# The end of a routing stage: four tiles taken together, and the order of the projections behind them

## The chip, the cores and the metric

The kernel runs on one core of one Trainium2 chip. The metric is the device time of one execution in microseconds (us), the median of several runs; less is better. A core has five engines that work side by side and meet only at semaphores: PE (matmuls and transposes; its weight loads are shown as PEld), DVE (vector), ACT (activations), POOL (here: memsets and storing DMAs) and SP (here: loading DMAs). Each engine runs its own list of instructions strictly in order.

## What is computed

The reference has two layers. The first routes 2048 states of width 256 over 1601 context tokens of width 192, and updates each state through a gated cell; the second is a transformer block (self-attention, cross-attention, MLP) on the result. Cut to what matters here:

```python
# layer 0
tok = ctx @ W_proj + b_proj
attn = softmax(x @ tok.T / 16)
routed = attn @ tok
ps_n, in_n = ln(x), ln(routed)
u = sigmoid([ps_n, in_n] @ W_u + b_u)
r = sigmoid([ps_n, in_n] @ W_r + b_r)
cand = tanh([r * ps_n, in_n] @ W_n + b_n)
x = ln((1 - u) * x + u * cand)
# layer 1
h = ln(x)
q, k, v = h @ Wq.T + bq, h @ Wk.T + bk, h @ Wv.T + bv     # 16 heads of 16
x = x + softmax(q k.T / 4) v @ Wo.T + bo                   # self-attention
x = x + cross_attention(ln(x), ctx)
x = x + gelu(ln(x) @ W1.T + b1) @ W2.T + b2
```

## The kernel before, in words

The 2048 rows are 16 tiles of 128 rows, and four chunks of four tiles. Layer 0 goes over the chunks; for each it computes scores against the 13 context tiles (`l0_scores`), their exponentials (`exps` on ACT), the low parts (`lower` on DVE) and the weighted sum of context (`l0_pv`). All that follows for a tile is a pipeline of stages, each written out by hand in every engine's list, one `slot(k)` for each k from 0 to 22. Tile k-4 is routed and normalised in slot k, tile k-5 goes through the gates and the candidate, tile k-6 is finished, and tile k-7 is normalised for layer 1.

For one tile the path is: `route` (PE, bank 6: the routed row and its softmax sum) → `norms` (DVE: reciprocal, scaling into E1, statistics, a `rsqrt` of twelve small instructions for up to three tiles at once, then the two normalised tiles XHS and XH1) → `hats` (PE: four transposes into bank 3) → `concat` (ACT: CF with scale and bias) → `gates` (PE: r and u into bank 7) → `reset` (ACT: tanh) → `gates` (DVE: UZ, RPS) → `update` (ACT: tanh) and `candidate` (PE, bank 7 again) → CZ (DVE) → `candidate` (ACT: tanh to CD) → the new state E2 with its statistics (DVE) → `finish` in the next slot (DVE) → the `rsqrt` and XH1 one slot later → `h_transposed` (PE, bank 2) → `h_taken` (ACT: hF). TR, RPS, UZ, TU, CZ, CD, E1 and E2 exist once, CF, XHS and XH1 twice.

Once the hF of a chunk's four tiles is there, its q, k and v are projected. `stage3` lists for each chunk ten units: keys of two halves, four v tiles, queries of two halves, and a norm of the keys and one of the queries (`norm`, a product of squares with a matrix of heads). For a q or k unit ACT makes three passes (`split`: two parts and a square), DVE makes the low part (`lower_parts`), and POOL stores both parts to DRAM (`store_parts`), from where SP loads them into the stacked layout of the attention. `qkv_bank` gives a unit its PSUM bank. DENSE, EARLY and LATE say in or behind which slot units stand: chunk 0 behind slot 10, chunk 1 (FIRST) in slots 16 and 17, chunk 2 (SECOND) in slots 19 to 21, chunk 3 behind slot 22. Slots 16 to 22 have no scores left beside the tail of the pipeline.

The self-attention starts after that. Its first scores (PE, `scores`) need the queries with their shift rows: once the key norm of the last chunk is known, DVE computes the shift (`self_shift(0)`, lines 1656, 1657, then `shift_rows`, lines 1518, 1519), POOL stores it (`store_shift`) and SP loads it. They also need `decide(0)`: after the last query norm DVE reduces the norms (L1834, L1835), PE turns the column into a row (L1228), DVE writes a flag (L1838, L1839), and every engine reads this flag into a register and branches on it (`general`). In the attention a pass of 928 exponentials on ACT (L886) and the products on PE (L1308 scores, L1325 values) run with double and triple buffering.

POOL fills half of V with ones in one memset of 4096 columns (L645) once the last `l0_pv` is done; DVE writes features of heads into it later. The lines of the profile are those of this file:

Of the kernel before, what the change touches and what calls it, by code (L numbers as in the profile page):

```python
# [131 lines left out]
def build(nc, ctx, d, out):  # L132
# [87 lines left out]
    TU = m.put("TU", [P, D], F32, oWOP + 3 * D * 4)  # L220
    PS = ctx.enter_context(nc.psum_tensor("PS", [P, 8, CHUNK], F32))
# [21 lines left out]
    AGX, NYX, MXP, NMX = 192, 224, 256, 272  # L243

    def sm(o, n=1, p=P):
# [10 lines left out]
        l0_scores l0_exp l0_lo l0_pv l0_oc l0_routed l0_hat l0_hatT l0_concat  # L256
# [44 lines left out]
    for n in range(CHUNKS):  # L301
        vs = [("v", kt, 0, 0) for kt in range(n * TPC, (n + 1) * TPC)]
        ks, qs = ([(kind, n * CHUNK, CHUNK, mm) for mm in range(2)] for kind in "kq")
        norms = [("norm", CHUNKS + 2 * n + i, CHUNK, 0) for i in range(2)]
        stage3.append([(10 * n + i,) + e for i, e in
                       enumerate(ks + vs[:2] + qs[:1] + norms[:1] + qs[1:] + vs[2:] + norms[1:])])
# [6 lines left out]
    DENSE = {10: 0, 22: 3}  # L313
    FIRST, SECOND = stage3[1], stage3[2]
    EARLY = {16: FIRST[0:4], 17: FIRST[8:10], 21: SECOND[8:10]}
    LATE = {16: FIRST[4:8], 19: SECOND[0:4], 20: SECOND[4:8]}
    SLOTS = TILES + TPC + 3
# [34 lines left out]
    def part_buffer(u):  # L352
# [5 lines left out]
        return PARTS[:, mm], S[f"parts_stored{mm}"], n  # L358

# [251 lines left out]
    def _(gp):  # L611
# [37 lines left out]
        for i in range(CHUNKS):  # L649
            store_shift(i, 0, i * CHUNK)  # L650
# [15 lines left out]
    def _(act):  # L666
        def split(u, bank, w, mm, bias):


            wait(act, S["parts_ready"], u - 1)  # L670
# [95 lines left out]
        def reset(i):  # L766

            act.wait_ge(S["l0_gates"], i + 1)
            wait(act, S["l0_rps"], i)
            for c in range(2):  # L770
                ins = act.activation(TR[:, c, :], PS[:, 7, c * P:(c + 1) * P], ACT.Tanh, bias=sm(BRH + c), scale=0.5)  # L771
            ins.then_inc(S["l0_rtanh"], 1)

        def update(i):

            act.wait_ge(S["l0_ubiased"], i + 1)
            act.activation(TU[:], UZ[:], ACT.Tanh, scale=0.5)

        def state_hat(i):
# [5 lines left out]
            act.activation(XHS[:, i % 2, 0, :], X[:, i, :], ACT.Identity, scale=sm(NYX + i), bias=sm(NMX + i))  # L785

        def concat(i):

            act.wait_ge(S["l0_hatT"], i + 1)
            for k, (g_, b_) in enumerate(2 * [("L0_xattn_g_state", "L0_xattn_beta_state")]  # L790
                                         + 2 * [("L0_xattn_g_input", "L0_xattn_beta_input")]):
                ins = act.activation(CF[:, i % 2, k, :], PS[:, 3, k * P:(k + 1) * P], ACT.Identity,  # L792
# [3 lines left out]
        def candidate(i):  # L796

            act.wait_ge(S["l0_candz"], i + 1)
            act.activation(CD[:], CZ[:], ACT.Tanh).then_inc(S["l0_cand"], 1)

        def slot(k):
# [4 lines left out]
            if b >= CHUNKS:  # L806
                if k == TILES:
                    routed_out(b - 1)
                if g is not None:
                    reset(g)  # L810
                qkv(EARLY.get(k, ()))
                if g is not None:
                    update(g)
                state_hat(tile_at(k, 3))
                if r is not None:
                    concat(r)
                if g is not None:
                    candidate(g)
                qkv(LATE.get(k, ()))
                if h is not None:  # L820
                    h_taken(h)
                return
# [26 lines left out]
            else:  # L849
                if j == TPC - 1 and b + 1 < CHUNKS:  # L850
                    shift_row(b + 1)
                state_hat(tile_at(k, 3))
# [7 lines left out]
        for k in range(SLOTS):  # L860
            slot(k)
            if k in DENSE:
                qkv(stage3[DENSE[k]])

# [56 lines left out]
    def _(pe):  # L921
# [164 lines left out]
        def route(i):  # L1086
# [6 lines left out]
            wait(pe, S["l0_hat"], i)  # L1093
            pe.matmul(PS[:, 6, 0:D + 1], OC[:, 0, tt * P:(tt + 1) * P], WN[:, 0, :], start=True, stop=False)
            pe.matmul(PS[:, 6, 0:D + 1], OC[0:SUM + 1, 1, tt * P:(tt + 1) * P], WN[0:SUM + 1, 1, :],
                      start=False, stop=True).then_inc(S["l0_routed"], 1)

        def hats(i):

            pe.wait_ge(S["l0_hat"], i + 1)  # L1100
            take(3, S["l0_concat"], i + 1)
            for k in range(4):
                ins = pe.transpose(PS[:, 3, k * P:(k + 1) * P], XHS[:, i % 2, k // 2, (k % 2) * P:(k % 2 + 1) * P],  # L1103
                                   ident[:])
            ins.then_inc(S["l0_hatT"], 1)

        def gates(i):

            pe.wait_ge(S["l0_concat"], i + 1)
            wait(pe, S["l0_candz"], i)  # L1110
            for mm in range(2):
                for c in range(4):
                    pe.matmul(PS[:, 7, mm * P:(mm + 1) * P], W0[:, 1, c, mm * P:(mm + 1) * P], CF[:, i % 2, c, :],  # L1113
                              start=(c == 0), stop=(c == 3))
            for c in range(4):
                ins = pe.matmul(PS[:, 7, D:2 * D], CF[:, i % 2, c, :], W0[:, 0, c, :], start=(c == 0), stop=(c == 3))  # L1116
            ins.then_inc(S["l0_gates"], 1)

        def candidate(i):
# [3 lines left out]
            pe.wait_ge(S["l0_rps"], i + 1)  # L1123
            for c in range(4):
                ins = pe.matmul(PS[:, 7, 0:D], RPS[:, c, :] if c < 2 else CF[:, i % 2, c, :], W0[:, 2, c, :],  # L1125
                                start=(c == 0), stop=(c == 3))
            ins.then_inc(S["l0_candps"], 1)

        def slot(k):
# [4 lines left out]
            if b >= CHUNKS:  # L1134
                if k == TILES:
                    for i in range(LAG):
                        l0_pv(n - LAG + i)
                    route(r)
                if g is not None:
                    gates(g)  # L1140
                qkv(EARLY.get(k, ()))
                if r is not None:
                    hats(r)
                if g is not None:
                    candidate(g)
                if tile_at(k, 3) is not None:
# [946 lines left out]
```

## Time and profile before

| | us |
|---|---|
| three runs | 1520.23, 1520.31, 1516.40 |
| their median | 1520.23 |
| the profiled execution, whole | 1512.68 |
| its span on the core | 1511.0 |
| mean granted PE clock in it, of full speed | 0.968 |
| last `l0_pv` of layer 0 issued | 322.4 |
| first score product of the self-attention | 435.24 |

All times of rows count from the start of the span. The span has a first part (layer 0 at full pace, up to about 322 us), the stretch from 322 to 435 us that holds slots 16 to 22 with the last projections, and the attentions with the MLP from 435 us on. In the rows a bracket after an instruction is the idle time of its engine just before it, and what ended that. PS is the whole PSUM, so the line tells which bank is meant; names that end in a number in the code have lost it in the rows (E is E1 or E2, XH is XH1).

### The profile page before, as it was taken

The page shows a single profiled execution, that of the slowest core. Times are in us where ns is not written, and L with a number is a line of the kernel's source. Part 1 is how long each engine was busy: PE and PEld are TensorE (multiplying, and loading weights), DVE is VectorE, ACT ScalarE, POOL GpSimd, SP SyncE. Part 2 cuts the span into 40 slices and gives each one's busy share as a digit, 9 for nine tenths or more (in the row PEclk, how much of TensorE's full clock was granted, in tenths as well). Part 3 has the DMA queues.
Part 4 walks back from the last instruction along what each step waited for, and adds up shares of the span by engine and source line. Part 5 has one row for each costly group of instructions (what it writes and reads, how often), then busy time and mean ns, then how long its engine had stood idle before and what let it go on. Part 6 is the DMA issues. An engine that isn't in the chain of part 4 may idle for free.

```text
span 1511.0 us, 20524 instructions
## 1 busy us (share of the span) xinstructions
PE 1409.6 (93%) x7934; PEld 623.1 (41%) x7934; DVE 567.5 (38%) x1343; ACT 1094.8 (72%) x1346; POOL 48.7 (3%) x63
## 2 busy tenths in 40 slices
PE   7989899996679999999999998998999999999988
PEld 5668676775422223223222322322323432432347
DVE  5557575777540113303322231440431233143132
ACT  2543444453359999998999998888877787788842
POOL 2000000010010000000000000000000000000000
PEclk9999999998789999999999999999899999999998
DMA  9410001001269000100100353501000000000000
GB/s 298 164 37 1 1 1 56 1 29 51 88 125 148 22 13 12 39 14 15 34 28 12 44 119 48 122 29 47 12 12 15 22 12 12 22 15 1 4 11 14
DMA packets 35048, 66.05 MB, mean 44 GB/s; under 512 B 6203, under 2 KB 20093, under 8 KB 34205
## 3 DMA queue, kind: packets, MB, share of 16 engines
q1 hardware_dynamic: 29580, 43.24, 13.3%
q0 software_dynamic: 5360, 21.37, 3.9%
q8 instruction: 69, 1.13, 0.3%
q14 instruction: 39, 0.31, 0.1%
HBM read 42.70 MB, written 22.02 MB: 43 GB/s over the span
## 4 chain that ended last, share of the span: by engine, by line
PE 67%; ACT 21%; DVE 6%; issue 3%; DMA 2%; SPq 0%; DVEq 0%; POOL 0%; ACTq 0%; POOLq 0%
PE PS L1325 20%; ACT PX L886 19%; PE PS L1308 14%; PE PS L1376 4%; PE PS L1386 3%; PE PS L1361 2%; PE PS L1113 2%; PE PS L1125 2%; PE PS L1116 2%; PE PS L1042 2%; PE PS L1081 1%; PE PS L1082 1%; PE PS L1083 1%; PE PS L1344 1%; PE PS L1459 1%
## 5 line engine op out<-in xcount | busy, mean ns | idle before, releaser
L886 ACT ACTIVATE PX<-PS 128x1024 f32<-128x1024 f32 (+1 forms) x928 | 882.6, 1039 | 136.0 <-PE PS L1308 87.9
L1325 PE MATMUL PS<-PX,V 128*32 128x512 f32 (+1 forms) x3712 | 500.7, 612 | 5.0 <-ACT PX L886 3.0
L1308 PE MATMUL PS<-QST,stack 50*128 50x512 f32 (+1 forms) x1856 | 386.0, 474 | 19.6 <-issue 13.7
L1308 PEld LDWEIGHTS PS<-QST,stack 50*128 50x128 f32 (+1 forms) x1856 | 157.0, 185 | 417.5 <-ACT PX L886 335.5
L1882 DVE COPY OT<-PS 128x512 f32<-128x512 f32 x32 | 22.1, 691 | 310.5 <-PE PS L1325 309.3
L1325 PEld LDWEIGHTS PS<-PX,V 128*32 128x32 f32 (+1 forms) x3712 | 73.9, 108 | 151.3 <-issue 129.3
L755 ACT ACTIVATE PH<-PS 128x512 fp32r<-128x512 f32 (+1 forms) x52 | 31.2, 600 | 79.4 <-PE PS L1062 69.3
L1386 PE MATMUL PS<-W,HIDT 128*128 128x256 f32 x192 | 51.5, 414 | 9.8 <-ACT HIDT L872 9.8
L1376 PE MATMUL PS<-HC,W 128*128 128x512 f32 x96 | 53.2, 641 | 0.0
L1909 DVE RECIPROCAL REC<-REC 128x256 f32<-128x256 f32 x30 | 52.6, 1753 | 1.0
L771 ACT ACTIVATE TR<-PS,small 128x128 f32<-128x128 f32 x32 | 10.0, 363 | 56.7 <-PE PS L1116 56.7
L1386 PEld LDWEIGHTS PS<-W,HIDT 128*128 128x128 f32 x192 | 36.5, 200 | 34.5 <-issue 30.0
L1954 DVE TENSOR_SCALAR HIDT<-PS,cols 128x512 f32<-128x512 f32 x24 | 18.0, 751 | 79.9 <-PE PS L1376 79.8
L1694 DVE TENSOR_TENSOR PL<-PEXP,PH 128x512 fp32r<-128x512 f32 (+1 forms) x52 | 35.8, 689 | 27.2 <-ACT PEXP L756 26.1
L1081 PE MATMUL PS<-PH,CN 128*128 128x512 f32 (+1 forms) x104 | 43.2, 416 | 0.9 <-DVE PL L1694 0.9
L1932 DVE TENSOR_TENSOR XH<-PS,rows 128x256 f32<-128x256 f32 x28 | 11.9, 425 | 81.2 <-PE PS L1361 81.2
L1082 PE MATMUL PS<-PH,CN 128*128 128x512 f32 (+1 forms) x104 | 41.5, 399 | 0.0
L1083 PE MATMUL PS<-PL,CN 128*128 128x512 f32 (+1 forms) x104 | 41.4, 398 | 0.0
L1587 DVE TENSOR_REDUCE small<-PS 128x1 f32<-128x512 f32 x64 | 35.1, 570 | 8.2 <-PE PS L963 7.4
L1959 DVE TENSOR_TENSOR XH<-PS,rows 128x256 f32<-128x256 f32 x12 | 5.1, 425 | 78.2 <-PE PS L1386 78.2
L1042 PE MATMUL PS<-hF,SAW 128*128 128x512 f32 x64 | 31.5, 627 | 2.0 <-ACT hF L736 2.0
L792 ACT ACTIVATE CF<-PS,cols 128x128 f32<-128x128 f32 x64 | 24.0, 456 | 10.6 <-PE PS L1103 10.6
(194 smaller groups left out, 1461.6 us busy)
## 6 DMA issues: line engine op xcount, KB each, us to landing
QST<-q_parts SPq DMA_DIRECT2D x192, 64.0 KB
q_parts<-PARTS POOLq DMA_DIRECT2D x16, 512.0 KB, 3.6
stack<-k_parts SPq DMA_DIRECT2D x24, 200.1 KB, 6.7
stack<-k_parts SPq DMA_DIRECT2D x18, 256.0 KB
k_parts<-KPARTS POOLq DMA_DIRECT2D x8, 512.0 KB, 3.2
v_cross<-V POOLq DMA_DIRECT2D x1, 3328.0 KB, 12.3
V<-v_cross SPq DMA_DIRECT2D x2, 1664.0 KB, 13.7
k_parts<-PARTS POOLq DMA_DIRECT2D x6, 512.0 KB, 3.4
```

The costliest lines, as they stand in the source:

```text
L886: act.activation(PX[0:kr, (2 * t + half) % 4, :, :], PS[0:kr, slot:slot + 2, :], ACT.Exp, scale=SCALE).then_inc(at["exp"], 1)
L1042: ins = pe.matmul(PS[:, bank, :], SAW[:, "qk".index(kind), c, mm * P:(mm + 1) * P], hF[:, c, at:at + w], start=(c == 0), stop=(c == 1))
L1081: pe.matmul(PS[0:w, bank, :], c_hi, hi, start=first, stop=False)
L1082: pe.matmul(PS[0:w, bank, :], c_lo, hi, start=False, stop=False)
L1083: ins = pe.matmul(PS[0:w, bank, :], c_hi, lo, start=False, stop=last)
L1308: ins = pe.matmul(PS[0:kr, 2 * (n % LOOK) + jj, :], KST[a][lo:lo + NROW, pair, kt * P:kt * P + kr].bitcast(F32R), QST[lo:lo + NROW, pair, ...
L1325: ins = pe.matmul(PS[32 * j:32 * j + 32, 6, :], V[0:kr, kt, 2 * (g // 2 * GH + j) + g % 2, :], PX[0:kr, (2 * t + j // 2) % 4, j % 2, :], s ...
L1376: ins = pe.matmul(PS[:, 7, :], (CAWQ if kind == "u" else W1)[:, c, i * P:(i + 1) * P], HC[:, c, :], start=(c == 0), stop=(c == 1))
L1386: ins = pe.matmul(PS[:, 7, 0:D], HIDT[:, k, i * P:(i + 1) * P], W2[:, k, :], start=(k == 0), stop=(k == HID // P - 1))
L1587: ve.tensor_reduce(sm(MXP + tt * len(pcs) + p), PS[:, max_bank(m), 0:pcs[p][1]], AX, ALU.max) \
L1694: ve.tensor_tensor(PL[0:kr, n % RING, :].bitcast(F32R), PEXP[0:kr, n % RING, :], PH[0:kr, n % RING, :], ALU.subtract).then_inc(S["l0_lo"], 1)
L1909: ch(ve.reciprocal(part, part))
```

## The change

The slots 16 to 22 are gone; in their place each engine has a list `last_tiles()`, in which the four tiles 12 to 15 go through each step together or closely behind each other.

- Tiles 12 to 15 get buffers of their own (CF4, XHS4, TR4, RPS4, TU4, CD4, E4), and banks of their own: routed rows in 6, 4, 5, 3 and gates in 6, 4, 5, 7.
- DVE takes statistics of the four routed rows straight from PSUM (`routed_stats`), folds the softmax sum into the scale with small instructions (`routed_scales`, one `rsqrt` over six columns), and ACT makes the four normalised rows (`routed_hat`) in the order 15, 12, 13, 14. The later `rsqrt`s run over one, one, four and four columns.
- DVE's list puts units of chunks 1 and 2 between the tiles' steps; PE's list too. Chunk 2's units use banks 4, 5, 6, 7, 1, 0 and the rest three or six banks instead of four.
- In every chunk the norm of the keys now stands ahead of both query units; DVE takes the last chunk's key norm and the shift before its v tiles, and the first shift skips one copy (L1656). POOL stores this shift ahead of the last queries.
- POOL's memset of half of V is now eight memsets, of the columns that DVE doesn't write, behind a wait for `l0_scaled`; DVE waits for each by itself.
- ACT's `split` no longer waits for `parts_ready`.

```diff
-            ks + vs[:2] + qs[:1] + norms[:1] + qs[1:] + vs[2:] + norms[1:]
+            ks + vs[:2] + norms[:1] + qs + vs[2:] + norms[1:]
-        return (0, 1, 2, 3)[u % 4] if u < 10 else (0, 1, 4, 5)[u % 4]
+        if u < 10:
+            return (0, 1, 2, 3)[u % 4]
+        return (u - 10) % 3 if u < 20 else (4, 5, 6, 7, 1, 0)[(u - 20) % 6]
 # POOL
-                gp.memset(V[:, TILES // 2:TILES], 1.0).then_inc(S["v_cleared"], 1)
+                gp.wait_ge(S["l0_scaled"], 1)
+                for n in range(TILES // 2, TILES):
+                    gp.memset(v_parts(n, P)[:, :, 1:3, :], 1.0).then_inc(S["v_cleared"], 1)
 ...
+                if half and i == CHUNKS - 1:
+                    store_shift(0, 0, 0)
 # ACT
+        def routed_hat(i):
+            j = i - FIRST_LAST
+            act.wait_ge(S["l0_scaled"], 1)
+            act.activation(XHS4[:, j, 1, :], PS[:, route_bank(i), 0:D], ACT.Identity, scale=sm(SC4 + j),
+                           bias=sm(SB4 + j)).then_inc(S["l0_hat"], 1)
+        def last_tiles():
+            a, b, c, e = LASTS
+            routed_out(CHUNKS - 1)
+            reset(a - 1)
+            update(a - 1)
+            for i in LASTS:
+                state_hat(i)
+            qkv(FIRST[0:2])
+            h_taken(a - 3)
+            for i in (e, a, b, c):
+                routed_hat(i)
+            candidate(a - 1)
+            concat(a)
+            concat(b)
 ...
+            qkv(SECOND)
+            for i in LASTS:
+                h_taken(i)
+            qkv(THIRD)
 # PE
+        def last_tiles():
+            a, b, c, e = LASTS
+            for i in range(LAG):
+                l0_pv(STEPS - LAG + i)
+            gates(a - 1)
+            for i in LASTS:
+                route(i)
+            candidate(a - 1)
+            qkv(FIRST[0:2])
+            h_transposed(a - 3)
+            qkv(FIRST[2:5])
+            hats(a)
+            hats(b)
+            gates(a)
+            hats(c)
+            gates(b)
+            candidate(a)
+            h_transposed(a - 2)
+            hats(e)
+            gates(c)
+            h_transposed(a - 1)
+            candidate(b)
+            gates(e)
+            qkv(FIRST[5:6])
+            candidate(c)
+            qkv(FIRST[6:8])
+            candidate(e)
+            qkv(FIRST[8:])
+            qkv(SECOND[0:8])
+            for i in LASTS:
+                h_transposed(i)
+            qkv(SECOND[8:])
+            qkv(THIRD)
 # DVE
+        def routed_stats(i):
+            j = i - FIRST_LAST
+            ve.wait_ge(S["l0_routed"], i + 1)
+            ch(ve.reciprocal(sm(RS4 + j), PS[:, route_bank(i), D:D + 1]))
+            stats(PS[:, route_bank(i), 0:D], j, ch, STAT4, AG4)
+        def last_tiles():
+            norms(None, a - 2, a - 3)
+            finish(a - 2, into=four[5])
+            gates(a - 1)
+            for i in LASTS:
+                routed_stats(i)
+            routed_scales()
+            next_hat(a - 2, AG4 + 10, NY4 + 5)
+            candidate_sum(a - 1)
+            new_state(a - 1, four[4])
+            rsqrt4(1, 4)
+            finish(a - 1, AG4 + 8, NY4 + 4, four[6])
+            gates(a)
+            qkv(FIRST[0:4])
+            gates(b)
+            candidate_sum(a)
+            qkv(FIRST[4:5])
+            new_state(a, four[0])
+            rsqrt4(1, 6)
+            next_hat(a - 1, AG4 + 12, NY4 + 6)
+            gates(c)
+            candidate_sum(b)
+            new_state(b, four[1])
+            gates(e)
+            candidate_sum(c)
+            qkv(FIRST[5:6])
+            new_state(c, four[2])
+            candidate_sum(e)
+            qkv(FIRST[6:8])
+            new_state(e, four[3])
+            rsqrt4(TPC)
+            finish(a, AG4, NY4, four[0])
+            qkv(FIRST[8:])
+            finish(b, AG4 + 2, NY4 + 1, four[1])
+            qkv(SECOND[0:2])
+            finish(c, AG4 + 4, NY4 + 2, four[2])
+            finish(e, AG4 + 6, NY4 + 3, four[3])
+            rsqrt4(TPC)
+            next_hat(a, AG4, NY4)
+            next_hat(b, AG4 + 2, NY4 + 1)
+            qkv(SECOND[2:5])
+            next_hat(c, AG4 + 4, NY4 + 2)
+            next_hat(e, AG4 + 6, NY4 + 3)
+            qkv(SECOND[5:])
+            qkv(THIRD[0:2] + THIRD[4:5] + THIRD[2:4] + THIRD[5:])
```

Here a, b, c, e are tiles 12, 13, 14, 15; `candidate_sum` is the addition that makes CZ, `new_state` the three instructions that make E2 and its statistics, `next_hat` the one that makes XH1.

## Rows read from the trace of the kernel before

**Rows 1.** The page: busy time of two engines, and PE's granted clock in 40 slices.
```profile
DVE  5557575777540113303322231440431233143132
...
PEclk9999999998789999999999999999899999999998
```

**Rows 2.** Windows: stretch, its length, busy time of PE, PEld, DVE, ACT, POOL; clock; DMA.
```profile
322.40:435.20 112.80, 76.45 (x318) 52.79 (x316) 73.80 (x226) 42.15 (x91) 13.24 (x15) 0.86 0.23 77
...
388.00:398.00 10.00, 8.29 (x32) 5.22 (x31) 6.90 (x17) 3.95 (x9) 1.45 (x2) 1.00 0.28 105
...
404.00:411.00 7.00, 2.15 (x6) 0.87 (x6) 5.19 (x19) 1.19 (x4) 1.42 (x2) 0.50 0.78 237
```

**Rows 3.** Timeline of DVE (start, us, engine, line, operation): one tile's period.
```profile
354.50 0.42 DVE L1746 TENSOR_TENSOR CZ<-PS,rows 128x256 f32<-128x256 f32 x1 [1.27 <-PE PS L1125]
355.48 0.42 DVE L1750 TENSOR_TENSOR E<-CD,X 128x256 f32<-128x256 f32 x1 [0.55 <-ACT CD L799]
...
357.75 0.17 DVE L1701 RECIPROCAL small<-PS 128x1 f32<-128x1 f32 x1
357.95 0.48 DVE L1702 TENSOR_SCALAR E<-PS,small 128x256 f32<-128x256 f32 x1
...
359.38 0.17 DVE L1496 TENSOR_SCALAR small<-small 128x3 f32<-128x3 f32 x1
...
361.77 0.41 DVE L1709 TENSOR_SCALAR XHS<-E,small 128x256 f32<-128x256 f32 x1
...
362.67 0.42 DVE L1723 TENSOR_TENSOR UZ<-PS,rows 128x256 f32<-128x256 f32 x1
...
363.59 0.48 DVE L1734 SCALAR_TENSOR_TENSOR E<-E,small,rows 128x256 f32<-128x256 f32 x1
...
367.19 0.43 DVE L1746 TENSOR_TENSOR CZ<-PS,rows 128x256 f32<-128x256 f32 x1 [1.70 <-PE PS L1125]
```

**Rows 4.** Timeline of DVE: its work for projected units, and the last XH1.
```profile
392.52 1.42 DVE L1536 TENSOR_TENSOR KPARTS<-KPARTS 128x512 fp32r<-128x512 f32 x2
...
404.84 0.75 DVE L1683 TENSOR_TENSOR V<-PS,rows 128x256 f32<-128x256 f32 x2
405.62 0.68 DVE L1672 COPY NQ<-PS 16x512 f32<-16x512 f32 x1
...
409.36 0.41 DVE L1714 TENSOR_SCALAR XH<-X,small 128x256 f32<-128x256 f32 x1
```

**Rows 5.** Timeline of PE: gates, candidates and the last keys, with idle time before them.
```profile
363.61 2.07 PE L1125 MATMUL PS<-W,RPS 128*128 128x256 f32 x4 [0.71 <-DVE RPS L1725]
...
386.99 1.89 PE L1116 MATMUL PS<-W,CF 128*128 128x256 f32 x8
390.60 1.13 PE L1125 MATMUL PS<-W,RPS 128*128 128x256 f32 x4 [1.71 <-DVE RPS L1725]
...
411.57 5.08 PE L1042 MATMUL PS<-hF,SAW 128*128 128x512 f32 x8 [1.05 <-ACT hF L736]
```

**Rows 6.** Timelines of DVE, PE, POOL: flag and first scores, twice, and the shift.
```profile
430.43 0.14 DVE L1839 TENSOR_SCALAR flag<-small 1x1 int32<-1x1 f32 x1
...
435.24 1.65 PE L1308 MATMUL PS<-QST,stack 50*128 50x512 f32 x6 [5.04 <-issue]
...
938.30 0.14 DVE L1839 TENSOR_SCALAR flag<-small 1x1 int32<-1x1 f32 x1
...
943.13 1.65 PE L1308 MATMUL PS<-QST,stack 50*128 50x512 f32 x6 [5.06 <-issue]
...
428.79 0.52 POOL L630 DMA_DIRECT2D shift<-Rp  x1 [0.26 <-issue]
```

**Rows 7.** Timeline of ACT: taking a transposed tile, and the first key pass of chunk 3.
```profile
410.62 0.81 ACT L736 ACTIVATE hF<-PS,cols 128x128 f32<-128x128 f32 x2 [4.12 <-PE PS L1024]
414.98 0.69 ACT L674 ACTIVATE KPARTS<-PS,cols 128x512 f32<-128x512 f32 x1 [3.55 <-PE PS L1042]
```

**Rows 8.** Timeline of POOL: the memset of half of V.
```profile
322.83 3.51 POOL L645 MEMSET V<- 128x4096 f32 x1 [82.52 <-PE PS L1083]
```

**Rows 9.** Windows: the start of the self-attention, columns as in rows 2.
```profile
435.00:500.00 65.00, 64.06 (x402) 18.86 (x402) 6.30 (x12) 62.61 (x68) 1.01 (x2) 0.95 0.82 130
```

More of the change, by code:

```diff
@@ L858, in slot @@
                 h_taken(h)
-        for k in range(SLOTS):
+        for k in range(TILES):
             slot(k)
@@ L1133, in slot @@
             n = LT * b + (3 * j + 1 if j else 0)
[L1134 to L1146, printed above, removed]
-                    route(r + 1)
-                qkv(LATE.get(k, ()))
-                if h is not None:
-                    h_transposed(h)
-                return
             if j == 0:
@@ L1207, in slot @@
             maxima(5)
-        for k in range(SLOTS):
+        for k in range(TILES):
             slot(k)
@@ L1726, in gates, with finish @@
                                     op0=ALU.add, op1=ALU.mult).then_inc(S["l0_rps"], 1)
             ve.wait_ge(S["l0_rps"], g + 1)
-        def finish(f):
+        def finish(f, mean=AG, y=NY, into=(2, STAT, AG)):
             if f is None:
                 return
-            xt = X[:, f, :]
-            ch(ve.scalar_tensor_tensor(out=E2[:], in0=E2[:], scalar=sm(AG), in1=row("L0_xattn_g_out"),
+            xt, e2 = X[:, f, :], work_of(f)[6]
+            ch(ve.scalar_tensor_tensor(out=e2, in0=e2, scalar=sm(mean), in1=row("L0_xattn_g_out"),
@@ new lines, in candidate_sum, with new_state @@
+        def candidate_sum(g):
+            ve.wait_ge(S["l0_candps"], g + 1)
+            ve.tensor_tensor(work_of(g)[4], PS[:, gate_bank(g), 0:D], row("L0_xattn_b_n"), ALU.add) \
+                .then_inc(S["l0_candz"], 1)
+            ve.wait_ge(S["l0_candz"], g + 1)
+        def new_state(g, into=(0, STAT, AG)):
+            ve.wait_ge(S["l0_cand"], g + 1)
+            _, _, _, tu, _, cd, e2 = work_of(g)
+            xt = X[:, g, :]
+            ch(ve.tensor_tensor(e2, cd, xt, ALU.subtract))
+            ch(ve.scalar_tensor_tensor(out=e2, in0=tu, scalar=1.0, in1=e2, op0=ALU.add, op1=ALU.mult))
+            ch(ve.scalar_tensor_tensor(out=e2, in0=e2, scalar=0.5, in1=xt, op0=ALU.mult, op1=ALU.add))
+            i, st, ag = into
+            stats(e2, i, ch, st, ag)
@@ new lines, in last_tiles @@
+        def last_tiles():
+            a, b, c, e = LASTS
+            four = [(j, STAT4, AG4) for j in range(7)]
+            norms(None, a - 2, a - 3)
[22 more added lines that the diff above has]
+            candidate_sum(c)
+            qkv(FIRST[5:6])
+            new_state(c, four[2])
[17 more added lines that the diff above has]
+            qkv(THIRD[0:2] + THIRD[4:5] + THIRD[2:4] + THIRD[5:])
@@ L1759, in slot @@
             n = LT * b + (3 * j + 1 if j else 0)
-            if b >= CHUNKS:
-                norms(r, f, h)
-                gates(g)
-                finish(f)
-                qkv(LATE.get(k - 1, ()))
-                qkv(EARLY.get(k, ()))
-                candidate(g)
-                return
             if j == 0:
@@ L1818, in slot @@
                 x_stats((None, range(6, 12), range(12, 16))[k])
-        for k in range(SLOTS):
+        for k in range(TILES):
             slot(k)
```

190 lines of the change are left out of this document (121 added, 69 removed).

## The prediction

> **What bounds the kernel now.** I read the page first: DVE is busy to 0.5 or more in the first slices only, and PE's clock is whole nearly everywhere [rows 1]; so most of the span is not what this change touches. The windows then show the stretch that it does: 322.4 to 435.2 us, 112.8 us, in which PE is busy 76 us, DVE 74 and ACT 42 [rows 2]. No engine is full: the stretch is a dependence chain that changes hands. DVE's timeline shows the pace. From one CZ to the next is 367.19 - 354.50 = 12.7 us, and inside one period DVE waits only where it handed work to PE or ACT and has its sole buffer in play (0.55 and 1.70 us) [rows 3]. All in all DVE idles 16.0 us between 323.05 (its first instruction of slot 16) and 409.77 (end of the last XH1 [rows 4]); the other 70.7 us it works, with its gaps of 0.03 us counted in. Then come the keys of chunk 3, 411.57 [rows 5], and the first scores, 435.24 [rows 6].
>
> What ends that last piece isn't what the chain of waits names, the load of the shift. Between flag and first scores lie 435.24 - 430.57 = 4.67 us at the self-attention, and 943.13 - 938.44 = 4.69 us at the cross-attention, where no shift was late [rows 6]. Two equal gaps: the flag, which each engine reads into a register and branches on, opens the attention. The shift only has to be in time.
>
> **The change, part by part.** The sum follows DVE's new list from 323.05 on, since DVE has the most work in it. Prices, each a difference of starts [rows 3]: new_state 357.75 - 355.48 = 2.27; a rsqrt 361.77 - 359.38 = 2.39; XH1 0.45; gates 363.59 - 362.67 = 0.92; finish 1.94 (as 2.27 without one operation, its two being 0.48 long); CZ 0.45; reciprocal with statistics 359.38 - 357.75 - 0.50 = 1.13, as the scaling of 0.48 goes. Units: low part 0.72, v tile 0.38, key norm 0.71, query norm 1.42 [rows 4].
>
> 1. DVE's work up to XH1 of tile 15. Six rsqrts (14.3), seven XH1 (3.15), six finishes (11.6), five gates (4.6), four routed statistics (4.5), four small scaling instructions (0.8), five CZ (2.25), five new states (11.4), and of chunks 1 and 2: six low parts (4.3), six v tiles (2.3), two key norms (1.4) and one query norm (1.4). Sum 62.0 us, against 70.7. The 8.7 that go: four scalings into E1 (2.0), four XHS that ACT makes now (1.8), one rsqrt (2.4), less the four small ones (0.8), is 5.4; about 3.6 is only moved (two low parts, two v, a query norm of chunk 2 behind XH1).
>
> 2. DVE's waits. I walked the three lists side by side with these prices, PE's gates at 3.5 us and a candidate at 1.73 (eight of 0.215 at full clock), a q or k unit at 1.72, concat 1.5, each of ACT's split 1.73. Waits that remain: 2.6 us before the new state of tile 11 (ACT stands in its split of two keys, tile 9 and four hats, then tanh); 0.3 and 0.9 at the gates of 12 and 13; 1.2 and 0.6 around CZ and tanh of 13, because PE holds its candidate behind h_transposed(11), which waits for DVE's XH1 of tile 11; 1.0 at the gates of 15; 1.8 and 0.9 at CZ of 14 and 15, where a query unit runs ahead of the candidate. Sum 9.3 against 16.0. PE idles 2.2 us before candidate 13. After an idle of 1.71 us the four products took 1.13, while behind 3.3 us and then 0.71 us they took 2.07 [rows 5]; 2.2 is nearer to the first, so I add 0.4 (ends 0 and 1.8). XH1 of tile 15 then ends at 323.05 + 62.0 + 9.3 + 0.4 = 394.8, 15.0 us earlier.
>
> 3. From there to chunk 3's keys. Four transposes share bank 2, so each waits for ACT to take the one before: 0.65 + 0.81 + 0.05 = 1.5 us [rows 7]. The first can start at 392.0, the fourth ends at 397.1, and ACT has it at 398.0. PE then issues two units of chunk 2 ahead of the keys, up to 2.7 us at the half clock; that spell would have cost k (5.08 us for two instead of 3.44 [rows 5]), so the keys come out as if started at 398.5. That is 3.7 us behind XH1 against 1.8: +1.9 us.
>
> 4. Chunk 3 up to the scores, 23.7 us before. Key norm and shift move ahead of the v tiles and the queries, one copy of 0.46 goes. Queries start one norm later (+0.3 at ACT) and DVE has no shift between q0 and q1. The last query norm hangs on ACT's square of q1 and comes out 2.0 us earlier: -2.0. Shift ready at +10.5, and by the row of POOL [rows 6] 6.45 us more plus 0.6 makes +17.6, under the flag's +21.6.
>
> Sum: -15.0 + 1.9 - 2.0 = -15.1 us.
>
> **At nothing.** Dense chunk 0: its norm waits for ACT's second key square either way; its q0 comes out 0.1 us later. POOL: its one memset took 3.51 us for 4096 columns [rows 8], and eight of 256 are 1.8 us; the new wait for the scales starts them near 336.5, and behind it on POOL stands the store of chunk 1's keys, ready near 349. Without this cover, 1.8 us at most. SP may load the first key quarters some 38 us earlier, since the last routed product moves from slot 19's end to 330; nobody waits for them. The dropped parts_ready wait of ACT is implied by the store's.
>
> The Trainium skill speaks against the memsets' place. SBUF — State Buffer, section "SBUF: two separate sides", says that DVE's two-port modes and GpSimd lock each other out for a whole instruction. XH1 of tile 10 is a tensor_scalar in SBUF and falls beside them. By that rule it would be late by one small piece, an estimate below 0.5 us, swallowed by the 2.6 us wait that follows; no row here shows such a lock.
>
> **The rivals.**
> (B) The handoffs cost more than walked. Every wait of item 2 is a small difference of two long paths. If they stay as in the kernel before (16.0 instead of 9.7 us), the gain is 8.8: 1511.4. For it: the old waits stand in the trace. Against it: own buffers and banks take away their cause.
> (C) They cost less, or the flag's gap shrinks to the shift's time. With the shift as gate, item 4 gives 23.7 - 17.6 = 6.1 instead of 2.0: gain 19.2, 1501. For it: the chain of waits names the shift; against it: the two equal gaps.
> (D) The gain is given back in the attention: key loads of later groups come late. The first 65 us of it have DMA at 0.82 and yet ACT busy 62.6 of 65 [rows 9], and the loads move with the start. Time: 1518 to 1520.
> (E) Slower: PE's clock. Between gates 12 and candidate 15 PE's products are on the path, some 29 us at full clock. Before, stretches with gaps ran at 0.50, and dense ones at 1.00 [rows 2]. At the half clock throughout they take 29 us more, minus 15.1 is +14: 1534. It decides at half of this stretch; with 20 of 29 us at half clock the time is 1525. For it: two gaps of 1.6 and 2.2 us remain. Against it: PE gets denser, and a gap of 1.71 cost 0.1 [rows 5].
> By TensorE: Matmul & The Clock Gate in the Trainium skill (Part 1) the clock follows recent activity and re-warms after bursts; that is how (E) would happen, and the 0.50 in 404 to 411 agrees.
>
> **How the numbers follow.** The profiled execution is 1512.68 us whole, 1511.0 in span; its time less 15.1 is 1497.6. The three runs' median is 1520.23, so the forecast is 1505.1; I take the difference over. Chances: forecast 0.50 (own range 1501 to 1509), B 0.20, C 0.17, D 0.08, E 0.05. A measurement of this kernel tells 0.3%, 4.6 us, from no change. A quarter of B could end inside it: faster 0.82, same 0.13, slower 0.05. The range goes from C with both its parts (1496) to B with half of its tail (1516), leaving out D, E and some of B.
>
> **What would show it.** XH1 of tile 15 near 395 and first scores near 420 on the new timeline; the scores 4.7 us behind the flag; DVE's idle time in the stretch near 9 us with the longest wait on ACT's CD of tile 11; the shift's load landing 2 to 4 us before the scores could use it; the span behind the first score as before, 1075.8 us. Wrong it is if that last length grows, if PE's clock from 342 to 372 is under 0.8, or if the four transposes wait for something other than bank 2.

## The result, and the profile after

The changed kernel took 1507.32 us (median of four runs, 1501.16 to 1508.82) against 1520.27 of the kernel before; the ratio is 0.9924 with a 95% interval of 0.9898 to 0.9951. Timed again beside other kernels it was 0.9910 (0.9890 to 0.9929). The forecast was 1505.1. Its profiled execution has a span of 1499.5 us, 11.5 less than before. A gain of 11 to 13 us is thus seen, but the first interval (7 to 16 us) is too wide to tell the forecast's 15.1 us from rival B's 8.8, and the second (11 to 17 us) speaks against B. Where the gain lies is read from the profiles.

The page of the changed kernel: busy shares in 40 slices, of the engines in rows 1.

```profile
DVE  5556676675630222303312231440431233143132
...
PEclk9999999999889999999999999999999999999999
```

The windows of the changed kernel, columns as in [rows 2]: its stretch from the last `l0_pv` to the first scores, and two spells in it.

```profile
322.99:425.93 102.94, 77.55 (x318) 53.79 (x317) 68.51 (x209) 44.76 (x96) 11.97 (x22) 0.87 0.28 92
...
338.00:342.00 4.00, 3.85 (x11) 2.91 (x12) 1.46 (x5) 2.22 (x6) 1.31 (x6) 0.60 0.00 0
360.00:368.00 8.00, 7.61 (x36) 6.72 (x37) 3.49 (x9) 1.77 (x5) 0.00 (x0) 0.79 0.01 2
```

Against [rows 2] the stretch is 10 us shorter, DVE works 5 us less in it, PE about as long as before (77.6 us against 76.5). The two spells have PE busy nearly throughout and a granted clock of 0.60 and 0.79 of full speed, so part of each ran at the lower of the two levels, 1.2 instead of 2.4 GHz; it is called the half clock below.

DVE's timeline in the changed kernel, the instructions before which it waited:

```profile
340.33 0.43 DVE L1866 TENSOR_TENSOR E<-CD,X 128x256 f32<-128x256 f32 x1 [2.32 <-ACT CD L854]
...
349.14 0.42 DVE L1834 TENSOR_TENSOR TU<-PS,rows 128x256 f32<-128x256 f32 x1 [2.32 <-ACT TR L816]
...
363.39 0.42 DVE L1857 TENSOR_TENSOR CD<-PS,rows 128x256 f32<-128x256 f32 x1 [2.13 <-PE PS L1211]
...
368.49 0.42 DVE L1834 TENSOR_TENSOR TU<-PS,rows 128x256 f32<-128x256 f32 x1 [1.89 <-ACT TR L816]
...
371.28 0.42 DVE L1857 TENSOR_TENSOR CD<-PS,rows 128x256 f32<-128x256 f32 x1 [1.90 <-PE PS L1211]
...
398.21 0.41 DVE L1824 TENSOR_SCALAR XH<-X,small 128x256 f32<-128x256 f32 x1 [0.25 <-PE PS L1103]
```

With four more, of 0.26 to 0.88 us each, the ten waits sum to 13.3 us. PE's timeline shows what stood behind the second, third and fourth row, idle time and then products at the half clock:

```profile
338.14 3.49 PE L1118 MATMUL PS<-SAW,hF 128*128 128x256 f32 x8 [2.43 <-ACT hF L779]
...
360.39 0.44 PE L1103 MATMUL PS<-ident,XH 128*128 128x128 f32 x2 [2.17 <-DVE XH L1824]
...
363.07 2.92 PE L1198 MATMUL PS<-CF,W 128*128 128x128 f32 x16
...
397.44 0.66 PE L1103 MATMUL PS<-ident,XH 128*128 128x128 f32 x2 [1.05 <-ACT hF L779]
...
403.88 4.68 PE L1121 MATMUL PS<-hF,SAW 128*128 128x512 f32 x8
```

The two v tiles take 3.49 us (1.89 at full clock, as at 408.40), the r products of a tile 2.92 instead of 1.95. The fourth row is the second of the last four transposes; it and the two behind it each waited 1.05 us for ACT to empty bank 2. DVE's flag ended at 420.74 and the first scores began at 425.93:

```profile
420.60 0.14 DVE L2028 TENSOR_SCALAR flag<-small 1x1 int32<-1x1 f32 x1
...
425.93 1.65 PE L1413 MATMUL PS<-QST,stack 50*128 50x512 f32 x6 [5.57 <-issue]
```

The milestones of one profile of each kernel follow, all in us. "Tiles" runs from the start of the last `l0_pv` product to the end of XH1 of tile 15; "to keys" from there to PE's keys of chunk 3; "flag" from there to the end of DVE's flag; "gap" from there to the first scores; "sum" is the four together, "rest" all behind.

| kernel | tiles | to keys | flag | gap | sum | rest |
|---|---|---|---|---|---|---|
| before | 87.4 | 1.8 | 19.0 | 4.67 | 112.9 | 1075.8 |
| changed | 75.7 | 5.3 | 16.9 | 5.19 | 103.0 | 1073.6 |
| changed, again | 75.7 | 5.2 | 16.9 | 4.97 | 102.8 | 1074.2 |
| gap1 | 74.7 | 5.0 | 16.6 | 4.97 | 101.3 | 1074.0 |
| gap2 | 72.2 | 5.3 | 15.8 | 4.98 | 98.3 | 1076.3 |
| flag_late | 73.8 | 5.3 | 18.2 | 6.78 | 104.0 | 1074.6 |
| order_only | 91.0 | 1.8 | 20.4 | 12.03 | 125.3 | 1073.2 |
| order_keys | 88.1 | 1.8 | 20.2 | 4.78 | 114.9 | 1076.7 |
| keys_late | 75.4 | 5.3 | 16.2 | 4.64 | 101.5 | 1076.8 |
| twobanks | 75.5 | 3.1 | 16.4 | 4.78 | 99.7 | 1076.9 |
| units_late | 73.9 | 5.2 | 16.1 | 5.12 | 100.4 | 1076.3 |
| memset_early | 76.4 | 5.0 | 16.7 | 4.47 | 102.6 | 1074.6 |
| all_keys | 68.6 | 4.1 | 16.8 | 4.80 | 94.2 | 1077.3 |
| best | 67.0 | 4.2 | 16.7 | 4.77 | 92.6 | 1076.9 |

What lies ahead of the last `l0_pv` took 322.0 to 328.0 us from run to run, so a single span says little about a change of a few us; the columns say more. Five profiles (changed, changed again, flag_late, keys_late, twobanks) have the same lists up to XH1 of tile 15 (but for twobanks' bank of the last transposes), and their "tiles" lies between 73.8 and 75.7: the column moves by about 2 us on its own. "Rest" moves too, between 1073.2 and 1077.3 over all kernels.

A good part of the 2 us can be seen. PE idles 2.17 us ahead of the transposes of tile 11 in all five. In the changed kernel the products behind that gap ran at a granted clock of 0.67 (360.66 to 365.83). In flag_late, whose edit comes much later, they ran at 1.00 (364.13 to 369.37), the candidate took 1.03 us for each four products and the r products 1.95:

```profile
363.86 0.44 PE L1103 MATMUL PS<-ident,XH 128*128 128x128 f32 x2 [2.17 <-DVE XH L1824]
364.13 1.03 PE L1211 MATMUL PS<-W,RPS 128*128 128x256 f32 x4
...
365.86 1.95 PE L1198 MATMUL PS<-CF,W 128*128 128x128 f32 x16
```

DVE's waits at CZ of 13 and at the gates of 15 are 1.41 and 0.96 us there, against 2.13 and 1.89 in the changed kernel and 3.03 and 0.96 in keys_late. So one and the same idle gap is followed by the half clock in one execution and not in another, and a change of "tiles" is best compared with a profile that had the same clock behind this gap.

### The profile page after: what moved, and what is told of

The parts are those of the page before. It is cut to its first block, busy times and chain, and to the rows that moved or that the text cites. A ratio compares the mean times of both kernels' runs of the same rounds, so it can differ in the third digit from the quotient of the medians.

```text
span 1499.5 us, 20495 instructions
## 1 busy us (share of the span) xinstructions
PE 1410.1 (94%) x7934; PEld 624.6 (42%) x7934; DVE 562.3 (38%) x1326; ACT 1097.2 (73%) x1350; POOL 47.4 (3%) x70
## 3 DMA queue, kind: packets, MB, share of 16 engines
q8 instruction: 69, 1.13, 0.3%
## 4 chain that ended last, share of the span: by engine, by line
PE 70%; ACT 20%; DVE 6%; issue 3%; DMA 0%; SPq 0%; DVEq 0%; ACTq 0%
PE PS L1430 22%; ACT PX L965 17%; PE PS L1413 15%; PE PS L1481 4%; PE PS L1491 3%; PE PS L1466 2%; PE PS L1198 2%; PE PS L1201 2%; PE PS L1211 2%; PE PS L1160 2%; PE PS L1161 1%; PE PS L1162 1%; PE PS L1449 1%; PE PS L1564 1%; PE PS L1586 1%
## 5 line engine op out<-in xcount | busy, mean ns | idle before, releaser
L1413 PE MATMUL PS<-QST,stack 50*128 50x512 f32 (+1 forms) x1856 | 385.4, 473 | 20.2 <-issue 13.9
L1198 PEld LDWEIGHTS PS<-CF,W 128*128 128x128 f32 x256 | 31.9, 197 | 1.8
```

Source lines behind the costliest of these rows:

```text
L1198: pe.matmul(PS[:, bank, mm * P:(mm + 1) * P], W0[:, 1, c, mm * P:(mm + 1) * P], cf[:, c, :], start=(c == 0), stop=(c == 3))
L1413: ins = pe.matmul(PS[0:kr, 2 * (n % LOOK) + jj, :], KST[a][lo:lo + NROW, pair, kt * P:kt * P + kr].bitcast(F32R), QST[lo:lo + NROW, pair, ...
```

## The experiments

**PE's gaps.** gap1 gives chunk 1's first units other banks, gap2 swaps one pair.

```diff
 # gap1
-        return (u - 10) % 3 if u < 20 else (4, 5, 6, 7, 1, 0)[(u - 20) % 6]
+        if u < 20:
+            return (0, 1, 0, 1, 7, 2, 0, 1, 2, 0)[u - 10]
+        return (4, 5, 6, 7, 1, 0)[(u - 20) % 6]
 # gap2, PE
-            h_transposed(a - 1)
             candidate(b)
+            h_transposed(a - 1)
 # gap2, ACT
-            h_taken(a - 1)
             candidate(b)
+            h_taken(a - 1)
```

> The changed kernel with one map altered: chunk 1's first two v tiles go to banks 0 and 1 (free once ACT has squared the keys) and its key norm to bank 7, instead of 2, 0 and 1, so PE no longer waits 2.43 us for ACT to take tile 9 out of bank 2. Theory (the time missing against the forecast is PE's idle gaps and the half clock behind them): the two v tiles take 1.7 to 1.9 us instead of 3.49, hats of tile 12 start near 339.0 instead of 341.9, DVE's wait at the gates of tile 12 falls from 2.32 to about 0.3 us, XH1 of tile 15 starts near 396.2 instead of 398.2 and the first scores near 423.9 instead of 425.9. Rival (the DVE waits only move on): XH1 of tile 15 stays within 0.5 us of 398.2.

> The changed kernel with one pair swapped on PE and on ACT: PE does the candidate of tile 13 ahead of the transposes of tile 11, ACT the tanh of tile 13 ahead of taking tile 11. PE then has no 2.17 us gap. Theory (gap and half clock): DVE's waits at CZ of 13 (2.13) and at the gates of 15 (1.89) go nearly to 0, the r products of gates 15 take 1.95 instead of 2.92, XH1 of tile 15 starts 3.5 to 4 us earlier, near 394.5, first scores near 422. Rival (the DVE waits only move on): within 0.5 us of the 398.2 and 425.9 of the changed kernel.

gap1's "tiles" fell by 1.0 us, half of what was expected. PE's timeline of gap1 shows what took the place of the gain:

```profile
340.76 1.13 PE L1120 MATMUL PS<-SAW,hF 128*128 128x256 f32 x4
342.50 1.13 PE L1120 MATMUL PS<-SAW,hF 128*128 128x256 f32 x4 [0.60 <-ACT SQ L721]
...
347.28 3.01 PE L1200 MATMUL PS<-CF,W 128*128 128x128 f32 x16
350.08 2.53 PE L1203 MATMUL PS<-W,CF 128*128 128x256 f32 x8
```

The v tiles are near full clock now (1.13 us each, 1.03 at best), and the gates of tile 12, behind them, take 5.3 us from start to end instead of 3.7: the slow spell has moved on to the next work. PE idles 0.60 us between the v tiles and 2.05 ahead of these gates, instead of 2.43 and 1.69. all_keys, which has the same banks, repeats it (5.2 us); best, where PE idles 0.39 and 1.74 us ahead of the two hats, has these gates at 3.5. In gap2 the second gap is nearly gone (0.44 us), the candidate of tile 13 follows the gates of 14 at once, "tiles" fell by 3.4 us and the sum by 4.7. Gap2 comes close to the theory (3.5 to 4), and exceeds the 2 us by which that column moves on its own; gap1 alone doesn't. The waits on DVE do not just move on. flag_late divides the 3.4 us: against its 73.8, with the gap but no half clock behind it, gap2 gains 1.5, so some 1.5 us were the idle time and some 1.9 the half clock of the changed kernel's profile (single executions, so rough).

**What opens the attention.** Three copies ahead of the flag's chain:

```diff
+            if a == 0:
+                for _ in range(3):
+                    ch(ve.tensor_copy(R[:], NQ[0:HEADS, :]))
             decide(a)
```

> The changed kernel with three copies of 16x512 (0.45 us each with their gap) on DVE ahead of the reduction that opens the flag's chain; the copies write a row that is rewritten behind them. Theory (the flag opens the attention): first scores come 1.35 us later, 5.2 us behind the flag as before. Rival (the shift's load opens it): it was issued at 417.2 and is not touched, so the first scores stay at 425.9 and the gap behind the flag shrinks to 3.8 us.

The flag came 1.35 us later (18.21 instead of 16.86 behind the keys). SP issued the shift's loads 4.8 us ahead of the flag's end (3.5 in the changed kernel; such a load took 1.53 us in the chain of the kernel before; its landing isn't shown here), and yet the first scores moved with the flag, which speaks against the shift. But they moved by more than the flag did: the gap grew to 6.78 us, which neither theory had.

**The order of units alone**, in the kernel before. Its edit is the part of the change that reads `norms[:1] + qs`, with the shift of chunk 3 ahead of DVE's v tiles and of POOL's query stores, and one copy less.

> The kernel before with the one part of the change that isn't the four tiles: key norms ahead of the queries in every chunk, in chunk 3 norm and shift ahead of DVE's v tiles, POOL's first shift store ahead of the last queries, one copy less. Slots 16 to 22 as before. Forecast of this part: chunk 3's keys to first scores 21.7 us instead of 23.7, everything before 411.6 within 0.5 us, so the span falls by 2.0 us and the timed runs can't tell it (ratio 0.9985 to 0.9995). Rival: the flag's chain is as long as before (23.7) since the last query norm still ends it, ratio 1.000; a second rival is a loss in slots 16 to 21, where queries now stand behind the norm and ACT's squares, of up to 1 us.

It was slower: ratio 1.0054 (1.0032 to 1.0075), 1524.18 us. "Flag" went up by 1.4 us instead of down by 2.0, and the gap to 12.03 us. The first has two rows: the keys of chunk 3 ran at the half clock for longer (6.41 us for the two halves against 5.08 in [rows 5]), and with the four banks of the kernel before the second query unit waits for a v tile that DVE now takes behind the shift. PE's timeline of order_only:

```profile
431.42 1.98 PE L1044 MATMUL PS<-hF,SAW 128*128 128x512 f32 x4 [1.61 <-DVE V L1686]
```

The second is the larger. The DMA queues between the end of the flag and the first scores tell it. Columns are packets, MB and share of the 16 DMA engines' time; q1 carries SP's loads. First the kernel before, then the changed one, flag_late, and order_only:

```profile
q1 hardware_dynamic: 97, 0.14, 11.1%
q8 instruction: 1, 0.02, 1.3%
```

```profile
q1 hardware_dynamic: 356, 0.84, 67.0%
q8 instruction: 1, 0.02, 1.2%
```

```profile
q1 hardware_dynamic: 252, 0.97, 92.7%
q8 instruction: 1, 0.02, 1.5%
```

```profile
q1 hardware_dynamic: 301, 1.60, 96.6%
q8 instruction: 1, 0.02, 0.9%
```

The gaps are 4.67, 5.19, 6.78 and 12.03 us. In each lies one packet of the instruction queue. An earlier shift lets SP pass on earlier to the keys of groups 1 to 3, six loads of 256 KB for each group. SP's timelines of the changed kernel, flag_late and order_only show when it issued the first six:

```profile
422.60 4.05 SPq L505 DMA_DIRECT2D stack<-k_parts  x6
```

```profile
424.43 2.65 SPq L505 DMA_DIRECT2D stack<-k_parts  x6
```

```profile
438.75 3.10 SPq L465 DMA_DIRECT2D stack<-k_parts  x6
```

That is 1.9 us behind the flag's end, 0.6 us behind it, and 0.7 us ahead of it: in these three the gap is the longer, the earlier these loads start. Windows of 0.1 us place the instruction queue's packet as well: 2.1 us behind the flag's end in the kernel before, 2.3 in the changed one, 3.4 in flag_late and 8.5 in order_only; the first scores follow it by 2.6, 2.9, 3.4 and 3.5 us. Of the 7.4 us by which the gap grew in order_only, 6.4 lie ahead of this packet. The next run takes the loads away:

```diff
                 load_key_quarter(CHUNKS - 1)
+                sp.wait_ge(A[0]["scores"], 1)
                 for g in range(1, GROUPS):
```

> The kernel with the unit order alone (order_only), and SP waits for the first score product before it loads the keys of groups 1 to 3. In order_only 12.0 us lay between the flag and the first scores, while the loading queue took 97% of the DMA engines; in the kernel before 4.67 us at 11%, in the changed one 5.19 us at 67%. Theory (behind the flag something comes by DMA, one packet of the instruction queue lies in this gap in each trace, and bulk key loads that SP starts ahead of the flag hold it up): the gap falls back to 4.6 to 4.8 us, the first scores come 7.3 us earlier than in order_only, span minus 7. Rival (the shift's load, or the queries' stacked rows, open the attention): the gap stays near 12. Second rival: the late loads of group 1 stall the second group, 33 us behind the first score, and the gain is given back there.

> The changed kernel with the same wait of SP (groups 1 to 3 of the keys behind the first score product). Theory: the gap between flag and first scores falls from 5.19 to 4.6 to 4.8 us. Rival: it stays at 5.2, and then the 0.5 us belong to something else.

In order_keys the gap is 4.78 us, and in the same place the queue now reads:

```profile
q1 hardware_dynamic: 23, 0.02, 1.1%
```

The timed ratio is 1.0007 (0.9991 to 1.0024), against 1.0054 with the loads in front. The second rival fell as well: "rest" is 1076.7, within the spread of the others. So key loads that start close to the flag cost up to 7.3 us, shown. That they do it by holding up a fetch of instructions is likely, since the packet in q8 came 6.4 us later and is back at 1.9 us behind the flag in order_keys, but isn't proved; no run took the fetch away, and holding the loads back also clears the way for other transfers. Against the shift and the last chunk's keys as the transfer speaks that in order_only SP had issued all of them by 438.0, 13 us ahead of the first scores.

order_only's own second rival, a loss of up to 1 us in slots 16 to 21, stays open. "Tiles" was 3.6 us longer than in the kernel before, and 0.7 us longer in order_keys, whose lists are the same there; the difference between the two shows that this column moves by about 3 us in these kernels. Both have waits of 0.26 and 0.43 us at a v tile and a query norm, twice, that the kernel before hasn't. In keys_late the gap is 4.64, as expected, yet twobanks and memset_early have 4.78 and 4.47 without that wait, so the 0.5 us of the changed kernel stay unsettled.

**From the last XH1 to the keys.** twobanks alternates banks 2 and 3; units_late takes chunk 2's first five units on DVE behind the last XH1.

```diff
 # twobanks, PE and ACT, bank of the layer-1 transpose
+        return 2 if i < FIRST_LAST else 2 + i % 2
 # units_late, DVE
             finish(b, AG4 + 2, NY4 + 1, four[1])
-            qkv(SECOND[0:2])
             finish(c, AG4 + 4, NY4 + 2, four[2])
 ...
             next_hat(b, AG4 + 2, NY4 + 1)
-            qkv(SECOND[2:5])
 ...
-            qkv(SECOND[5:])
+            qkv(SECOND)
```

> The changed kernel with the last four layer-1 transposes in banks 2 and 3 by turns instead of bank 2 alone. In the changed kernel 5.3 us lie between the end of XH1 of tile 15 (398.62) and the start of chunk 3's keys (403.88), of which the four transposes and their takings wait for each other 1.05 us each. Theory (the single bank serialises them): the last transpose starts near 399.2 instead of 400.86, the keys 1.5 us earlier. Rival (the two units of chunk 2 ahead of the keys, 2.6 us at half clock, set it): the keys move by less than 0.5 us.

> The changed kernel with five units of chunk 2 (two low parts, two v tiles, a key norm: 2.9 us of DVE) taken behind the last XH1 instead of among the finishes. Theory (DVE sets the path to XH1 of tile 15): XH1 of 15 starts 2.9 us earlier, 395.3, and the keys of chunk 3 and the first scores come 1.5 to 2.9 us earlier. Rival: PE's last two units of chunk 2 wait for these v tiles' banks (6 and 7), and the whole is given back before the keys.

twobanks took 2.1 us off "to keys" (5.26 to 3.11), more than the 1.5 expected, and its rival falls. units_late took 1.8 us off "tiles" (2.9 expected), within the 2 us by which that column moves; twobanks, with the same waits at CZ of 13 and the gates of 15 (2.08 and 1.94 us), has 75.5, so against it the gain is 1.6. What is missing shows on DVE's timeline: XH1 of tiles 14 and 15 now wait 0.15 and 1.20 us for PE's transposes out of the two XH1 buffers, which queue up at bank 2. Nothing was given back before the keys, 5.2 as before.

**The memset.**

```diff
-                gp.wait_ge(S["l0_scaled"], 1)
-                for n in range(TILES // 2, TILES):
-                    gp.memset(v_parts(n, P)[:, :, 1:3, :], 1.0).then_inc(S["v_cleared"], 1)
+                gp.memset(V[:, TILES // 2:TILES], 1.0).then_inc(S["v_cleared"], 1)
```

> The changed kernel with the memset of the kernel before: one of 4096 columns right behind the last l0_pv, no wait for the scales. XH1 of tile 10, a tensor_scalar from SBUF to SBUF, took 0.55 us in the changed kernel, where the eight small memsets run beside it, and 0.41 us everywhere else. Theory (the two engines share a port to SBUF there): it takes 0.41 us, and 0.14 us is all that the memsets' place costs; the stretch to the first scores is otherwise unchanged, since a wait of 2.3 us follows. Rival: 0.55 us stays, or the 3.5 us memset slows other instructions of DVE between 323 and 327 us.

Both halves hit something. XH1 of tile 10 took 0.41 us again, and one of the twelve small instructions of a rsqrt took 3.30 instead of 0.17. Timelines of POOL and DVE in memset_early:

```profile
323.36 3.51 POOL L685 MEMSET V<- 128x4096 f32 x1 [82.50 <-PE PS L1160]
...
323.59 3.30 DVE L1599 TENSOR_SCALAR small<-small 128x3 f32<-128x3 f32 x1
326.93 0.17 DVE L1600 TENSOR_SCALAR small<-small 128x3 int32<-128x3 int32 x1
```

The DVE instruction starts within the memset and ends 0.02 us behind the memset's end at 326.87. "Tiles" grew by 0.7 us only: XH1 of tile 10 came 3.1 us later, but the waits for CD of tile 11, at CZ of 13 and at the gates of 15 shrank by 0.6, 0.7 and 0.9. Only the first of these is slack that took up the delay. The other two waits, 1.41 and 0.96 us, are those of flag_late: in this execution too PE's clock was full behind the gap of 2.17 us. Against flag_late's 73.8 the 76.4 are 2.6 us more, which is the 3.1 less the 0.6. In the kernel before the same memset cost nothing that the trace shows, since DVE waited for PE during 2.14 of its 3.51 us and then mostly read from PSUM.

**All together**, timed on one chip with the changed kernel. all_keys has gap1, gap2, twobanks, units_late and keys_late; best has two more moves:

```diff
 # ACT
+            candidate(a - 1)
             for i in (e, a, b, c):
                 routed_hat(i)
-            candidate(a - 1)
 # DVE
-            gates(a)
             qkv(FIRST[0:4])
+            gates(a)
             gates(b)
```

> The changed kernel unaltered, timed beside the next two on one chip. It fixes how much of the stretch between last l0_pv and first scores (102.99 us in its first profile) is the run's own: theory and rival both expect a ratio to the kernel before of 0.990 to 0.995 and the stretch within 2 us of 103.

> The changed kernel with the edits of gap1, gap2, twobanks, units_late and keys_late together. Theory (PE's gaps with their half clock, then DVE's work, then bank 2, then the key loads ahead of the flag are links of one chain, so what they cost adds up): last l0_pv to end of XH1 of tile 15 near 69 us instead of 75.7, to the keys 3.1 to 3.6, to the flag 16.2, to the scores 4.7: 93.5 us instead of 103.0, ratio to the kernel before 0.985 to 0.988. Rival (they overlap: each alone took away the same slack): 98 us, ratio 0.989 to 0.991.

> all_keys with two more moves: ACT does the tanh of tile 11 ahead of the four routed hats, and DVE takes the first four units of chunk 1 ahead of the gates of tile 12 instead of behind them. Theory: of the waits of 2.3 us at CD of tile 11 and 1.5 to 2.5 us at the gates of tile 12 that are left, 1.9 and 1.5 go; XH1 of tile 15 comes 2 to 3.5 us earlier than in all_keys, first scores too, ratio to the kernel before 0.983 to 0.986. Rival (PE's list bounds by then): within 1 us of all_keys.

| kernel | median of the runs | ratio to before, 95% interval |
|---|---|---|
| changed, again | 1502.40 | 0.9910 (0.9890 to 0.9929) |
| all_keys | 1495.20 | 0.9857 (0.9834 to 0.9879) |
| best | 1494.14 | 0.9850 (0.9826 to 0.9873) |

all_keys' sum is 94.2 us where 93.5 was expected and 98 by the rival: the costs add up in the main. Compared with changed-again, "tiles" fell by 7.1 (gap1, gap2 and units_late alone: 1.0, 3.4 and 1.8), "to keys" only by 1.2, to 4.1 us where 3.1 to 3.6 were expected: PE waited 0.78 us for one of the v tiles that units_late moved behind XH1, which was that run's rival. The interval of its ratio leaves out the rival's 0.989 to 0.991. best beats both kernels, but its step over all_keys is 1.6 us in the profile and not to be told in the timed runs. The wait for CD fell from 2.31 to 0.55 us; the one at the gates of 12 grew from 1.50 to 2.59, though DVE comes to it with two low parts and two v tiles already done. PE is late there: it waits for ACT's concat of tile 12 ahead of the next hats, and ACT makes this behind the tanh that was moved forward.

```profile
341.78 0.63 PE L1195 MATMUL PS<-ident,XHS 128*128 128x128 f32 x4 [1.74 <-ACT CF L854]
```

## Why the prediction was right, step by step

The direction and the place were as forecast, and DVE's shorter list was the mechanism; the gain was 11.5 us between the two profiles and 13.0 between the medians, against 15.1. That it came so close is in part luck: the stretch that the change touches gave 9.9 us (112.9 to 103.0), nearer to rival B's 8.8 than to 15.1, and 2.2 us came from "rest", which no part of the forecast shortened. The second profile of the changed kernel has 10.1 and 1.6. Where the medians' remaining 2 to 3 us lie isn't shown. In the forecast's own terms: 15.1, plus 0.3 from DVE's work, less 3.6 for its waits, 1.4 between XH1 and the flag (1.2 of it the clock in chunk 3's keys), 0.5 for the gap and 0.6 ahead of slot 16, plus the 2.2, is 11.5.

1. **DVE's work** in the stretch was put at 62.0 us. By the changed kernel's rows it is 398.62 - 323.64 - 13.3 = 61.7. This is what the gain rests on, and it was right.
2. **DVE's waits** were put at 9.3, with 0.4 for PE's clock; they are 13.3. This is the term that was mis-sized, by 3.6 us. CD of tile 11 (2.6 said, 2.32 measured), the gates of 13 (0.9, 0.75) and CZ of 14 and 15 (1.8 and 0.9, 1.90 and 0.88) came out. The gates of 12 (0.3, 2.32), CZ of 13 (1.2, 2.13) and the gates of 15 (1.0, 1.89) did not, and each stands behind products at half speed. The step priced the clock for one of PE's two gaps, choosing for 2.2 us of idle the row with 1.71 us (1.13 for four products) over that with 3.3; it priced the other gap, 2.43 us ahead of the v tiles, at nothing. The two v tiles behind it then took 3.49 us. gap2 gave back 3.4 us by closing one gap, some 1.5 of them idle time and some 1.9 the half clock, if flag_late is taken for the same gap at full clock. So 0.4 was within what this gap can cost from one execution to another (0 in flag_late, 1.9 here); its range of 0 to 1.8 was better than its value.
3. **To the keys**, +1.9 was said, +3.5 came (5.26 against 1.80). The last three of the four transposes in one bank did wait 1.05 us each, as walked, and twobanks puts the one bank at 2.1 us. The term that failed is the credit of 1.6 us for the keys at full clock: the low clock carried on into them, and the two halves took 4.68 us, not 3.44 (5.08 before).
4. **Keys to flag**, -2.0 said, -2.1 came, 0.4 of it in the keys themselves. order_only shows that this was right for the changed kernel only: with four banks the same order lost 1.4 us.
5. **The flag opens the attention.** flag_late bears this out against the shift, and (C) falls. That the gap is fixed at 4.7 us was wrong: two equal gaps were taken for a constant, while both had few loads beside them. For the changed kernel that cost 0.5 us at most; the same step would have been wrong by 7.4 for order_only. The step that failed is "the shift only has to be in time": an earlier shift also starts, sooner, what is queued behind its load on SP.
6. **At nothing.** XH1 of tile 10 was said to be late by under 0.5 us beside the memsets; it took 0.55 instead of 0.41, so 0.14. The eight memsets took 2.22 us, not 1.8. What the prediction missed is that their new place is worth something: in the old one a rsqrt stands 3.1 us in the changed kernel, and memset_early puts that at some 2.6 us of the path. The Trainium skill (SBUF — State Buffer, "SBUF: two separate sides") says that a GpSimd instruction and a DVE one in a two-port mode lock each other out: whichever starts first holds the shared ports for its whole instruction. The 3.30 us of the small instruction, which started 0.23 us behind the memset and ended with it, agree. The 0.14 us do not plainly: by the trace XH1 started first, at 336.99, and the first memset at 337.09.

Of the sum the rest, 1075.8 to 1073.6, is the runs' own, as is 0.6 us ahead of slot 16. (B) put the waits back at 16.0; they were 13.3, midway between it and the forecast's 9.7, and the gain of the stretch was nearly B's. (D) and (E) did not show: the rest didn't grow, the clock over the stretch was 0.87 against 0.86, and from 342 to 372 us, where the sign of (E) was a clock under 0.8, it was 0.94.

## What to carry to other kernels

When tiles are taken together, sum the new list of the busiest engine for its work, and walk the others only for the waits; then price every idle gap of PE on that walk twice, as the gap and as the slow products that may stand behind it, and take the second price as a range, since it differs from one execution to the next. Before you read a gain of a few us from two profiles, see whether the same gaps had the same clock behind them. Moving a small transfer earlier moves everything that is queued behind it, so look at what that collides with, and hold bulk loads back until a step on which everything waits is through. A memset on POOL is best placed by what DVE runs beside it, not only by when it may start.

## What the runs showed of the hardware

- A DVE tensor_scalar on three columns in SBUF took 3.30 us instead of 0.17 beside a POOL memset of 3.51 us and was done 0.02 us behind it (memset_early, one execution); one of 256 columns took 0.55 us instead of 0.41 beside memsets of 256 columns (changed kernel).
- Between a flag written by DVE and the first instruction that depends on its branch lay 4.5 to 5.2 us in twelve profiles with SP's loads at up to 67% of the DMA engines' time, 6.8 us (flag_late) at 93% and 12.0 us (order_only) at 97%. The one packet of the instruction queue in this gap came 2.1 and 2.3 us behind the flag in the kernels before and changed, 3.4 and 8.5 us in these two.
- Behind an idle gap of PE of 2.17 us the granted clock was 0.67 in the changed kernel and 1.00 in flag_late, whose lists are the same up to there; in "tiles" that is 75.7 against 73.8 us.
- In gap1 the v tiles regained full speed, and the next tile's gates, behind 2.05 us of idle time, lost it (5.3 us instead of 3.7).
